# Two expert layers around a linear recurrence: the second layer's outputs added to the stored residual by accumulating scatters

## The chip, the cores and the metric

One core of a Trainium2 chip runs the whole program. The metric is the device time of one execution in microseconds. The kernel before took 563.17 us in the median of three runs (560.38 to 563.6).

## What is computed

The input is 4 sequences of 1024 tokens with 128 channels in float32. Three steps follow one another, each with a layer norm ahead of it and a residual around it: an expert layer with the better two of 8 experts for each token, a linear recurrence along the sequence, and the same expert layer again.

```python
x = x + 0.5 * moe(layernorm(x))
x = x + lru(layernorm(x))
x = x + 0.5 * moe(layernorm(x))

def moe(x):
    logits = x @ router_w.T + router_b
    topk_val, topk_idx = jax.lax.top_k(logits, 2)
    weights = jax.nn.softmax(topk_val, axis=-1)
    # for each of a token's two experts
    h = x @ w1[e].T + b1[e]; h1, h2 = split(h, 2)
    out = (silu(h1) * h2) @ w2[e].T + b2[e]
    return sum(weights * out)          # over the two experts
```

## The kernel before, in words

Each engine has a program of its own, written by hand, and semaphores tie them together; nothing reorders instructions, so the order in the code is the order on each engine. The residual stands in the on-chip buffer `xres` during the whole program. A layer number `f` (0 or 1) names the expert layer.

An expert layer works as follows. For each of the four sequences (`g`), PE makes the router's logits, DVE picks the two experts and works out a slot for each token and expert (`choose`, `row_weights`, `slots`). POOL then scatters the normalised tokens into a table in memory, `rows_dram[f]`, sorted by expert (`send_row`, line 436, 16 scatters of 128 rows for a sequence). A row is 130 words: the token as two float16 halves, its destination row (word `P`) and its weight (word `P + 1`). The table is cut into 39 tiles (`NTILE`) of 256 rows, each with rows of one expert; rows without a token are pads whose destination lies out of bounds, so a scatter leaves them out.

For each tile SP loads the tokens (transposed, line 363), destinations and weights (`meta`, line 367) and the bias (line 373). PE multiplies up and, two tiles later (`LAG`), down; ACT and DVE make the gated activation between them; ACT weights the result into one of eight buffers of `yout` (`weighted`, line 588). POOL sends these to memory (`send_y`, line 454): two scatters of 128 rows of 512 bytes, `r` = 0 and 1, to `y_dram[f]`, which has a row for each token and each of its two choices. The second scatter also waits until PE is three tiles further (`apart`). ACT fills a buffer again when the scatters of eight tiles before have landed (`s_ysent`). In the second layer two row scatters stand behind the outputs of each of tiles 0, 1 and 2, and eight behind those of each of tiles 5 and 6 (`BURSTS`). These are the rows of the third and fourth sequences that are still to be sent. The fourth sequence (`LATE`) is routed while the first 17 tiles (`KNOWN`), which hold the other three, are already being worked on.

When all outputs of a layer have landed, SP loads them back into `yin` (line 397, two loads of 512 KB for each sequence), DVE adds them to `xres` (`add_outputs`, line 967, two additions for each sequence), and, in the second layer alone, SP stores `xres` to `out` (line 402). The recurrence in between adds its part to `xres` on DVE in `add_recurrence` (line 1005) and raises `s_x2` for each sequence.

Of the kernel before, what the change touches and what calls it, by code (L numbers as in the profile page):

```python
# [6 lines left out]
FP32 = mybir.dt.float32  # L7
FP16 = mybir.dt.float16
I32 = mybir.dt.int32
ACT = mybir.ActivationFunctionType  # L10
ALU = mybir.AluOpType
AX = mybir.AxisListType.X

P = 128
BATCH, SEQ = 4, 1024
TOK = BATCH * SEQ
GT = SEQ // P
NE, HID, TOPK = 8, 512, 2
# [15 lines left out]
STEP = 4  # L34
BURSTS = {5: 8, 6: 8}
METAS, OUTS = 16, 8
# [4 lines left out]
LATE = BATCH - 1  # L41
# [4 lines left out]
KNOWN = WHOLE[LATE - 1]  # L46
# [8 lines left out]
def macaron_block(nc, x, nu_log, theta_log, b_re, b_im, c_re_t, c_im_t, d_vec, gamma_log,  # L55
                  router_t, router_b, w1_t, b1_t, w2_t, b2, out):
    ctx = ExitStack()
    with ctx:
# [3 lines left out]
        def sem(name):  # L62
            return ctx.enter_context(nc.semaphore(name))


        rows_dram = [nc.dram_tensor(f"rows{f}", [NE * REG + SLOT, ROWW], FP32, kind="Internal").ap() for f in range(2)]
        y_dram = [nc.dram_tensor(f"y{f}", [TOPK * TOK, P], FP32, kind="Internal").ap() for f in range(2)]


        xres = sb("xres", [P, BATCH, GT, P])  # L70
# [169 lines left out]
        s_cx = sem("s_cx")  # L240
        s_x2 = sem("s_x2")
        s_x3 = sem("s_x3")
        s_out = sem("s_out")

# [11 lines left out]
        def sent_before(f, tile, ring=STEP):  # L258

            count = lambda n: (n - tile % ring + ring - 1) // ring  # L260
            return f * count(NTILE) + count(tile)
# [51 lines left out]
        @block.sync  # L313
        def _(sp):
            route = [(rwt[:, :], router_t), (rbb[:, :], router_b.partition_broadcast(P))]
            small = [(b1g[:, :, :], b1_t), (b2b[:, 0, :], b2.partition_broadcast(2)),
                     (b_pow[:, 0, 0, :], b_re), (b_pow[:, 1, 0, :], b_im), (c_pow[:, 0, 0, :], c_re_t), (c_pow[:, 1, 0, :], c_im_t),
                     (vec[:, 0:1], nu_log), (vec[:, 1:2], theta_log), (vec[:, 3:4], d_vec), (vec[:, 2:3], gamma_log)]
            for g in range(BATCH):
                for c in range(2):  # L320
                    ts = slice(c * GT // 2, (c + 1) * GT // 2)
                    sp.dma_start(xres[:, g, ts, :], x[g].rearrange("(p t) d -> p t d", p=P)[:, ts, :])\
                        .then_inc(s_xin[g], 16)
                if g == 0:
                    for dst, src in route:
                        sp.dma_start(dst, src).then_inc(s_route, 16)
            for e in range(NE):
                if e == STAGED:
                    for dst, src in small:
                        sp.dma_start(dst, src).then_inc(s_small, 16)  # L330
                if e >= STAGED:

                    sp.wait_ge(s_wl, 2 * (e - STAGED + 1))
                sp.dma_start(wst[:, e % STAGED, 0:2 * HID], w1_t[:, e, :]).then_inc(s_w[e % STAGED], 16)
                sp.dma_start(wst[:, e % STAGED, 2 * HID:], w2_t[:, e, :]).then_inc(s_w[e % STAGED], 16)

            for f in range(2):

                sp.wait_ge(s_tab, f + 1)

                def pad(e):
                    row0 = sp.value_load(pad_i[0:1, f, e:e + 1], min_val=0, max_val=NE * REG - SLOT)
                    sp.dma_start(rows_dram[f][bass.ds(row0, SLOT), :].rearrange("(p r) w -> p r w", r=2),
                                 padrow[:, :, :]).then_inc(s_pad, 16)

                def pad_end():
                    sp.dma_start(rows_dram[f][NE * REG:NE * REG + SLOT, :].rearrange("(p r) w -> p r w", r=2),
                                 padrow[:, :, :]).then_inc(s_pad, 16)

                def load(t, n, dma):  # L350
                    if f > 0 and t == KNOWN:

                        sp.wait_ge(s_tab, 3)
                    row0 = sp.value_load(toff_i[0:1, f, t:t + 1], min_val=0, max_val=NE * REG)  # L354
                    if t in FIRST_OF:

                        sp.wait_ge(s_sent[FIRST_OF.index(t)], 16 * TOPK * GT * (f + 1))
                    if t == FIRST_OF[BATCH - 1]:

                        sp.wait_ge(s_pad, 16 * (NE + 1) * (f + 1))  # L360

                    wait(sp, s_up[HB - 1], n(1 - STEP))
                    sp.dma_start_transpose(xt_t[:, t % STEP, :, :], halves_dram[f][bass.ds(row0, SLOT), 0:2 * P])\  # L363
                        .then_inc(s_xt[t % STEP], 16)

                    wait(sp, s_ysent[t % OUTS], 32 * sent_before(f, t + OUTS - METAS, OUTS))
                    sp.dma_start(meta[:, t % METAS, :, :],  # L367
                                 rows_dram[f][bass.ds(row0, SLOT), P:].rearrange("(r p) w -> p r w", p=P))\
                        .then_inc(s_meta[t % STEP], 16)
                    expert = sp.value_load(tex_i[0:1, f, t:t + 1], min_val=0, max_val=NE - 1)  # L370

                    wait(sp, s_act[HB - 1], n(1 - STEP))
                    sp.dma_start(bias[:, t % STEP, :].unsqueeze(1), b1g[:, bass.ds(expert, 1), :])\  # L373
                        .then_inc(s_bias[t % STEP], 16)
                    if f > 0 and t == KNOWN - NE:

                        sp.wait_ge(s_ends, 1)
                    first_pad = STEP if f == 0 else KNOWN - NE
                    if first_pad <= t < first_pad + NE:
                        pad(t - first_pad)  # L380
                    if t == STEP:
                        pad_end()

                sp.wait_ge(s_b1u, 1)
                expert_tiles(f, load)

                if f == 0:
                    sp.wait_ge(s_turn, 1)
                for t in range(NTILE - OUTS, NTILE):
                    sp.wait_ge(s_ysent[t % OUTS], 32 * (sent_before(f, t, OUTS) + 1))  # L390
                for g in range(BATCH):
                    n = f * BATCH + g
                    if n >= 2:

                        sp.wait_ge(s_x1, n - 1)
                    for k in range(TOPK):
                        sp.dma_start(yin[:, n % 2, k, :, :],
                                     y_dram[f].rearrange("(k b p t) d -> k b p t d", k=TOPK, b=BATCH, p=P)[k, g])\
                            .then_inc(s_yin[n % 2][k], 16)
            for g in range(BATCH):  # L400
                sp.wait_ge(s_x1, BATCH + g + 1)
                sp.dma_start(out[g].rearrange("(p t) d -> p t d", p=P), xres[:, g, :, :]).then_inc(s_out, 16)
            sp.wait_ge(s_out, 16 * BATCH)


        @block.gpsimd
        def _(pool):
# [29 lines left out]
                    out=rows_dram[f], out_offset=bass.IndirectOffsetOnAxis(ap=slot_i[:, k, f, g, t:t + 1], axis=0),  # L437
                    in_=rows[:, k, g, t, :], in_offset=None).then_inc(s_sent[g], 16)

            last_row = pool.to_reg(TOPK * TOK - 1)  # L440

            def apart(t, j, n):

# [3 lines left out]
            def send_y(f, t, n):  # L447

                pool.wait_ge(s_yout, n(1))
                pool.sem_inc(s_ygo, 1)  # L450
                for r in range(2):
                    if r == 1:
                        apart(t, 0, n)
                    pool.indirect_dma_start(  # L454
                        out=y_dram[f],
                        out_offset=bass.IndirectOffsetOnAxis(ap=meta_i[:, t % METAS, r, 0:1], axis=0),
                        in_=yout[:, t % OUTS, r, :], in_offset=None, bounds_check=last_row,
                        oob_is_err=False).then_inc(s_ysent[t % OUTS], 16)

            for f in range(2):  # L460
                each = [(g, i) for g in range(BATCH) for i in range(TOPK * GT)]
# [181 lines left out]
        def _(dve):  # L643
# [8 lines left out]
            def linked(ins):  # L652

                count[0] += 1
                ins.then_inc(s_chain, 1)
                done = count[0]
                yield
                dve.wait_ge(s_chain, done)
# [110 lines left out]
            def row_weights(f, g):  # L769
                q = f * BATCH + g  # L770
                if (f, g) == (1, LATE):
                    yield from exponential(edif[:, q % 2, :], dif[:, q % 2, :], GT)
                else:

                    dve.wait_ge(s_edif, q + 1)
                yield from linked(V.tensor_scalar(den[:, :], edif[:, q % 2, :], 1.0, 2.0 * WS * WS, ALU.add, ALU.mult))
                yield from linked(V.reciprocal(wk[:, 0, :], den[:, :]))
                yield from linked(V.tensor_tensor(wk[:, 1, :], wk[:, 0, :], edif[:, q % 2, :], ALU.mult))
                for k in range(TOPK):
                    ins = V.tensor_copy(rows[:, k, g, :, P + 1:P + 2], wk[:, k, :].unsqueeze(2))  # L780
                yield from linked(ins)
# [329 lines left out]
            for f in range(2):  # L1111
# [31 lines left out]
                act_low(NTILE - 1, 1, lambda u: f * NTILE + NTILE - 1 + u)  # L1143
                for _ in late if f > 0 else tables:
                    pass
            for g in range(BATCH):
                add_outputs(1, g)


        @block.tensor  # L1150
# [263 lines left out]
```

## Time and profile before

| | us |
|---|---|
| median of three runs | 563.17 |
| the profiled execution, its own time | 563.79 |
| its span | 562.1 |
| busy in the span: PE, DVE, ACT, POOL | 451.9, 424.5, 359.0, 300.2 |

The engines are PE (matrix products), DVE (vectors), ACT (activations), POOL (which issues the indirect transfers) and SP (which issues the others). The profile is of one execution; its times are microseconds from the start of the span, and L454 is line 454 of the kernel before. A timeline row gives start, duration, engine, line, operation and, in brackets, how long the engine sat idle before it and what ended that. Landing is the time from the start of the issuing instruction until the transfer's semaphore is raised.

### The profile page before, as it was taken

The page shows a single profiled execution, that of the slowest core. Times are in us where ns is not written, and L with a number is a line of the kernel's source. Part 1 is how long each engine was busy: PE and PEld are TensorE (multiplying, and loading weights), DVE is VectorE, ACT ScalarE, POOL GpSimd, SP SyncE. Part 2 cuts the span into 40 slices and gives each one's busy share as a digit, 9 for nine tenths or more (in the row PEclk, how much of TensorE's full clock was granted, in tenths as well). Part 3 has the DMA queues.
Part 4 walks back from the last instruction along what each step waited for, and adds up shares of the span by engine and source line. Part 5 has one row for each costly group of instructions (what it writes and reads, how often), then busy time and mean ns, then how long its engine had stood idle before and what let it go on. Part 6 is the DMA issues. An engine that isn't in the chain of part 4 may idle for free.

```text
span 562.1 us, 15920 instructions
## 1 busy us (share of the span) xinstructions
PE 451.9 (80%) x4657; PEld 396.7 (71%) x4657; DVE 424.5 (76%) x1368; ACT 359.0 (64%) x797; POOL 300.2 (53%) x307
## 2 busy tenths in 40 slices
PE   7770269989899999987789986699987999999900
PEld 3660148768799999983689885488876889999900
DVE  8988658676879997744999998679965677777624
ACT  4896337666768877870607653578775688888700
POOL 1277876777864544551000477757677745454530
PEclk9555569999999999999688997799999999999955
DMA  8334433433334232316200011343344333333148
GB/s 286 121 110 141 114 83 93 102 98 93 73 76 72 54 65 57 64 25 218 82 1 1 31 53 49 86 80 86 78 107 93 87 70 66 58 66 63 28 147 301
DMA packets 94563, 50.27 MB, mean 89 GB/s; under 512 B 81902, under 2 KB 84720, under 8 KB 94484
## 3 DMA queue, kind: packets, MB, share of 16 engines
q1 hardware_dynamic: 85396, 32.31, 24.1%
q0 software_dynamic: 9088, 16.94, 9.7%
q8 instruction: 45, 0.74, 0.6%
q14 instruction: 34, 0.28, 0.2%
HBM read 17.25 MB, written 23.24 MB: 72 GB/s over the span
## 4 chain that ended last, share of the span: by engine, by line
PE 25%; SPq 24%; DVE 15%; POOL 13%; issue 11%; DMA 10%; ACT 2%; POOLq 0%; ACTq 0%; DVEq 0%
POOL rows L436 12%; SPq L363 9%; PE bank L1298 5%; PE bank L1300 5%; PE bank L1299 5%; SPq L373 4%; DMA xt_t<-rows 3%; SPq L367 3%; DMA yin<-y 3%; SPq L370 3%; SPq L354 3%; PE bank L1318 2%; PE bank L1319 2%; PE bank L1320 2%; DVE wst L1082 2%
## 5 line engine op out<-in xcount | busy, mean ns | idle before, releaser
L454 POOL DMA_INDIRECT y<-yout,meta x156 | 161.5, 1035 | 118.2 <-ACT yout L588 82.9
L1082 DVE SCALAR_TENSOR_TENSOR wst<-bank,bias,wst 128x256 f32<-128x256 f32 x312 | 148.6, 480 | 82.3 <-ACT wst L570 77.9
L1298 PE MATMUL bank<-xt_t,w1h 128*128 128x256 f16 x624 | 174.1, 279 | 43.1 <-DMA xt_t<-rows 26.9
L436 POOL DMA_INDIRECT rows<-rows,slot_i x128 | 136.6, 1068 | 120.6 <-DVE slot_i L797 81.6
L570 ACT ACTIVATE wst<-bank,bias 128x256 f32<-128x256 f32 x312 | 145.4, 474 | 74.5 <-PE bank L1300 42.0
L1299 PE MATMUL bank<-xt_t,w1h 128*128 128x256 f16 x624 | 173.9, 279 | 0.0
L1300 PE MATMUL bank<-xt_t,w1l 128*128 128x256 f16 x624 | 173.7, 278 | 0.0
L1318 PE MATMUL bank<-w2h,wst 128*128 x624 | 122.3, 220 | 1.0 <-DVE wst L1088 0.8
L1320 PE MATMUL bank<-w2h,wst 128*128 x624 | 120.2, 219 | 0.0
L1319 PE MATMUL bank<-w2l,wst 128*128 x624 | 120.2, 219 | 0.0
L1088 DVE TENSOR_TENSOR wst<-wst 128x512 f16<-128x512 f32 x156 | 107.8, 691 | 5.9 <-ACT wst L578 5.4
L578 ACT CAST wst<-wst 128x512 f16<-128x512 f32 x156 | 95.6, 613 | 16.1 <-DVE wst L1082 12.7
L1298 PEld LDWEIGHTS bank<-xt_t,w1h 128*128 x624 | 62.3, 100 | 53.1 <-issue 47.0
L491 ACT ACTIVATE xn<-xres,shift,rstd 128x128 f32<-128x128 f32 x96 | 38.2, 482 | 58.9 <-DVE shift L730 58.9
L1300 PEld LDWEIGHTS bank<-xt_t,w1l 128*128 x624 | 62.5, 100 | 8.6
L1318 PEld LDWEIGHTS bank<-w2h,wst 128*128 128x128 f16 x624 | 61.0, 98 | 7.8 <-issue 4.8
L1299 PEld LDWEIGHTS bank<-xt_t,w1h 128*128 x624 | 62.4, 100 | 4.7
L1319 PEld LDWEIGHTS bank<-w2l,wst 128*128 128x128 f16 x624 | 61.0, 98 | 2.3
L1320 PEld LDWEIGHTS bank<-w2h,wst 128*128 128x128 f16 x624 | 61.0, 98 | 0.0
L588 ACT ACTIVATE yout<-bank,meta 128x128 f32<-128x128 f32 x156 | 48.5, 364 | 2.7 <-PE bank L1320 2.6
L967 DVE TENSOR_TENSOR xres<-xres,yin 128x1024 f32<-128x1024 f32 x16 | 19.6, 1224 | 27.5 <-DMA yin<-y 27.0
L1162 PE MATMUL bank<-ident,xn 128*128 128x128 f32 x96 | 18.0, 329 | 10.3 <-ACT xn L491 10.0
(205 smaller groups left out, 509.3 us busy)
## 6 DMA issues: line engine op xcount, KB each, us to landing
yin<-y SPq DMA_DIRECT2D x16, 512.0 KB, 4.6
wst<-in_w_t SPq DMA_DIRECT2D x8, 512.0 KB, 5.0
y<-yout,meta POOLq DMA_INDIRECT x156, 2.4
rows<-padrow SPq DMA_DIRECT2D x18, 130.0 KB
xres<-in_x SPq DMA_DIRECT2D x8, 256.0 KB, 4.5
wst<-in_w_t SPq DMA_DIRECT2D x8, 256.0 KB, 5.7
rows<-rows,slot_i POOLq DMA_INDIRECT x128, 2.4
out<-xres SPq DMA_DIRECT2D x4, 512.0 KB, 6.9
```

Of the source, the lines that this page charges most:

```text
L436: pool.indirect_dma_start(out=rows_dram[f], out_offset=bass.IndirectOffsetOnAxis(ap=slot_i[:, k, f, g, t:t + 1], axis=0), in_=rows[:, k, g ...
L454: pool.indirect_dma_start(out=y_dram[f], out_offset=bass.IndirectOffsetOnAxis(ap=meta_i[:, t % METAS, r, 0:1], axis=0), in_=yout[:, t % OU ...
L570: nc.scalar.activation(gate[:, j, :], up_bank(f, t, j)[:, 0:SLOT], ACT.Silu, scale=1.0 / WS, bias=bias[:, t % STEP, j:j + 1]).then_inc(s_g ...
L578: nc.scalar.copy(acth[:, t % BUFS, 2 * half:2 * half + 2, :], act[:, 2 * half:2 * half + 2, :]).then_inc(s_acth[half], 1)
L1082: V.scalar_tensor_tensor(act[:, j, :], up_bank(f, t, j)[:, SLOT:], bias[:, t % STEP, HB + j:HB + j + 1], gate[:, j, :], ALU.add, ALU.mult) ...
L1088: V.tensor_tensor(actl[:, t % BUFS, h2, :], act[:, h2, :], acth[:, t % BUFS, h2, :], ALU.subtract).then_inc(s_actl[half], 1)
L1298: T.matmul(o, w1h[:, bass.ds(at, P)], xt_t[:, t % STEP, 0, :], start=True, stop=False)
L1299: T.matmul(o, w1h[:, bass.ds(at, P)], xt_t[:, t % STEP, 1, :], start=False, stop=False)
L1300: ins = T.matmul(o, w1l[:, bass.ds(at, P)], xt_t[:, t % STEP, 0, :], start=False, stop=True)
L1318: T.matmul(o, acth[:, t % BUFS, c, rs], w2h[:, bass.ds(at, P)], start=False, stop=False)
L1319: T.matmul(o, acth[:, t % BUFS, c, rs], w2l[:, bass.ds(at, P)], start=False, stop=False)
L1320: ins = T.matmul(o, actl[:, t % BUFS, c, rs], w2h[:, bass.ds(at, P)], start=False, stop=(c == HB - 1 and r == 1))
```

## The change

In the second layer the outputs don't go to a table of their own any more. The residual is stored to `out` beforehand: sequences 0 to 2 by SP between the layers, each when the recurrence has been added to it, and sequence 3 by SP behind the load of tile 4 (`base`). POOL's scatters then add to the rows of `out`. Both choices of a token go to the same row, so two tiles may hit one row, and the first scatter of a tile waits until both scatters of the tile before have landed. The first tile also waits for the stores of sequences 0 to 2, tile 17 for that of sequence 3. The destination of a token's second choice is set to the row of its first by one copy more on DVE for each sequence. The loads into `yin`, the additions and the stores at the end of the second layer go away; SP ends with the wait for the last eight tiles' scatters. The first layer stays as it was.

```diff
-        y_dram = [nc.dram_tensor(f"y{f}", [TOPK * TOK, P], FP32, kind="Internal").ap() for f in range(2)]
+        y_dram = nc.dram_tensor("y0", [TOPK * TOK, P], FP32, kind="Internal").ap()
+        sums = out.rearrange("b s d -> (b s) d")
...
+                def base(g):
+
+                    sp.wait_ge(s_x2, g + 1)
+                    sp.dma_start(out[g].rearrange("(p t) d -> p t d", p=P), xres[:, g, :, :]).then_inc(s_base[g], 16)
+
...
+                    if f > 0 and t == STEP:
+                        base(LATE)
...
-                for g in range(BATCH):
-                    n = f * BATCH + g
-                    if n >= 2:
-
-                        sp.wait_ge(s_x1, n - 1)
-                    for k in range(TOPK):
-                        sp.dma_start(yin[:, n % 2, k, :, :],
-                                     y_dram[f].rearrange("(k b p t) d -> k b p t d", k=TOPK, b=BATCH, p=P)[k, g])\
-                            .then_inc(s_yin[n % 2][k], 16)
-            for g in range(BATCH):
-                sp.wait_ge(s_x1, BATCH + g + 1)
-                sp.dma_start(out[g].rearrange("(p t) d -> p t d", p=P), xres[:, g, :, :]).then_inc(s_out, 16)
-            sp.wait_ge(s_out, 16 * BATCH)
+                if f == 0:
...
+                    for g in range(LATE):
+                        base(g)
...
-            last_row = pool.to_reg(TOPK * TOK - 1)
+            last_row = [pool.to_reg(TOPK * TOK - 1), pool.to_reg(TOK - 1)]
...
+                if f > 0:
+                    for g in range(BATCH):
+                        if t == (KNOWN if g == LATE else 0):
+
+                            pool.wait_ge(s_base[g], 16)
+                    if t > 0:
+
+                        pool.wait_ge(s_ysent[(t - 1) % OUTS], 32 * (sent_before(f, t - 1, OUTS) + 1))
...
-                        out=y_dram[f],
+                        out=sums if f else y_dram,
...
-                        in_=yout[:, t % OUTS, r, :], in_offset=None, bounds_check=last_row,
-                        oob_is_err=False).then_inc(s_ysent[t % OUTS], 16)
+                        in_=yout[:, t % OUTS, r, :], in_offset=None, bounds_check=last_row[f],
+                        oob_is_err=False, compute_op=ALU.add if f else ALU.bypass).then_inc(s_ysent[t % OUTS], 16)
...
+                if f > 0:
+                    V.tensor_copy(rows[:, 1, g, :, P:P + 1].bitcast(I32), dest_i[:, 0, g, :].unsqueeze(2))
...
-            for g in range(BATCH):
-                add_outputs(1, g)
```

POOL's queue in the second layer, before, from tile 5's outputs to tile 7's; `rows1` is the second layer's table, `y1` its outputs, and brackets name the semaphores that an instruction waits for:

```order
L454 DMA y1<-yout,meta 8192x128 [waits s_yout]
L454 DMA y1<-yout,meta 8192x128 [waits s_up0]
L436 DMA rows1<-rows,slot_i 35072x130 [waits s_slot,s_up1]
L436 DMA rows1<-rows,slot_i 35072x130 [waits s_up2]
L436 DMA rows1<-rows,slot_i 35072x130 x6
L454 DMA y1<-yout,meta 8192x128 [waits s_yout]
L454 DMA y1<-yout,meta 8192x128 [waits s_up0]
L436 DMA rows1<-rows,slot_i 35072x130 [waits s_row,s_up1]
L436 DMA rows1<-rows,slot_i 35072x130 [waits s_up2]
L436 DMA rows1<-rows,slot_i 35072x130 x6
L454 DMA y1<-yout,meta 8192x128 [waits s_yout]
L454 DMA y1<-yout,meta 8192x128 [waits s_up0]
```

The same place on POOL after the change, where the outputs go to `out_0`:

```order
L468 DMA out_0<-yout,meta 4096x128 [waits s_yout,s_ysent4]
L468 DMA out_0<-yout,meta 4096x128 [waits s_up0]
L442 DMA rows1<-rows,slot_i 35072x130 [waits s_slot,s_up1]
L442 DMA rows1<-rows,slot_i 35072x130 [waits s_up2]
L442 DMA rows1<-rows,slot_i 35072x130 x6
L468 DMA out_0<-yout,meta 4096x128 [waits s_yout,s_ysent5]
L468 DMA out_0<-yout,meta 4096x128 [waits s_up0]
L442 DMA rows1<-rows,slot_i 35072x130 [waits s_row,s_up1]
L442 DMA rows1<-rows,slot_i 35072x130 [waits s_up2]
L442 DMA rows1<-rows,slot_i 35072x130 x6
L468 DMA out_0<-yout,meta 4096x128 [waits s_yout,s_ysent6]
L468 DMA out_0<-yout,meta 4096x128 [waits s_up0]
```

Nothing has moved on POOL; each tile's first scatter has a second wait, for the scatters of the tile before (`s_ysent4` is tile 4's).

SP's queue at the end of the program, before, from the last tile's load of `meta`:

```order
L367 DMA meta<-rows1 128x2x2
L370 TENSOR_LOAD tex_i
L370 ISA x2
L373 ISA [waits s_act3]
L373 DMA bias<-b1g 128x8
L397 DMA yin<-y1 128x1024 [waits s_ysent4,s_ysent3,s_ysent5,s_ysent2,s_ysent6,s_ysent1,s_x1,s_ysent0,s_ysent7]
L397 DMA yin<-y1 128x1024
...
L397 DMA yin<-y1 128x1024 [waits s_x1]
L397 DMA yin<-y1 128x1024
L402 DMA out_0<-xres 128x1024 [waits s_x1] x4
L58 UNCONDITIONAL_BRANCH [waits s_out]
```

And after the change:

```order
L373 DMA meta<-rows1 128x2x2
L376 TENSOR_LOAD tex_i
L376 ISA x2
L379 ISA [waits s_act3]
L379 DMA bias<-b1g 128x8
L58 UNCONDITIONAL_BRANCH [waits s_ysent3,s_ysent4,s_ysent2,s_ysent5,s_ysent1,s_ysent6,s_ysent0,s_ysent7]
```

Eight loads and four stores are gone from SP's end; the wait for the last eight tiles' scatters stays and now stands ahead of the program's end.

## Rows read from the trace of the kernel before

**Rows 1.** Busy time by engine in stretches; us, then PE to POOL, clock, DMA
```profile
core 0 of [0], span 562.1 us
core 0: us, PE busy (x) PEld busy (x) DVE busy (x) ACT busy (x) POOL busy (x), PEclk, DMA share, GB/s
541.00:562.10 21.10, 0.00 (x0) 0.00 (x0) 9.80 (x8) 0.00 (x0) 0.00 (x0) 0.50 0.83 299
```

**Rows 2.** The chain that ended last, its end: start, duration, engine or transfer
```profile
538.62 2.15 DMA y<-yout,meta
...
541.79 5.74 DMA yin<-y
...
557.10 1.22 DVE xres L967
```

**Rows 3.** Line 402, the stores of out: duration in ns, first and last start
```profile
L402 SPq DMA_DIRECT2D out<-xres x4: 332/381/430, 550.9 to 558.4; - x4
...
DMA to landing us min/median/max: 3.3/6.9/7.6
```

**Rows 4.** Timeline of POOL in the second layer, around tiles 6 to 16
```profile
422.17 0.96 POOL L436 DMA_INDIRECT rows<-rows,slot_i  x1 [0.30 <-issue]
423.43 1.00 POOL L454 DMA_INDIRECT y<-yout,meta  x1 [0.30 <-issue]
...
450.57 0.98 POOL L454 DMA_INDIRECT y<-yout,meta  x1 [1.88 <-ACT yout L588]
```

**Rows 5.** Timeline of ACT, the outputs of tile 7 and of tile 30
```profile
403.90 0.62 ACT L588 ACTIVATE yout<-bank,meta 128x128 f32<-128x128 f32 x2
...
506.33 0.63 ACT L588 ACTIVATE yout<-bank,meta 128x128 f32<-128x128 f32 x2
```

**Rows 6.** Timeline of POOL, the two scatters of tile 30 and the next
```profile
507.75 0.98 POOL L454 DMA_INDIRECT y<-yout,meta  x1 [1.80 <-ACT yout L588]
509.04 0.98 POOL L454 DMA_INDIRECT y<-yout,meta  x1 [0.30 <-issue]
511.82 0.98 POOL L454 DMA_INDIRECT y<-yout,meta  x1 [1.80 <-ACT yout L588]
```

**Rows 7.** Line 454 in 425 to 450, then landings in 475-500 and 500-541
```profile
L454 POOL DMA_INDIRECT y<-yout,meta x17: 982/993/1474, 424.7 to 447.7; - x17
...
DMA to landing us min/median/max: 2.4/2.5/2.6
...
DMA to landing us min/median/max: 2.5/2.6/2.8
...
DMA to landing us min/median/max: 2.1/2.1/2.1
```

**Rows 8.** Timeline from 313 us: copies on DVE and the scatter they release
```profile
313.11 0.24 DVE L780 COPY rows<-wk 128x8 f32<-128x8 f32 x2
313.26 0.24 DVE L797 CAST slot_i<-slot 128x8 int32<-128x8 f32 x2
...
313.77 0.96 POOL L436 DMA_INDIRECT rows<-rows,slot_i  x1 [58.61 <-DVE slot_i L797]
```

**Rows 9.** Timeline of SP's queue: a pad, the next tile's load, tile 17's load
```profile
371.68 0.59 SPq L347 DMA_DIRECT2D rows<-padrow  x1
372.97 1.22 SPq L363 DMA_TRANSPOSE xt_t<-rows  x1
...
437.02 1.27 SPq L363 DMA_TRANSPOSE xt_t<-rows  x1
```

**Rows 10.** DMA queues (packets, MB, share of 16 engines) and issues (us to landing)
```profile
q0 software_dynamic: 9088, 16.94, 9.7%
...
y<-yout,meta POOLq DMA_INDIRECT x156, 2.4
...
rows<-rows,slot_i POOLq DMA_INDIRECT x128, 2.4
...
rwt<-in_router_t SPq DMA_DIRECT2D x1, 4.0 KB, 2.6
```

More of the change, by code:

```diff
@@ L242, in macaron_block @@
         s_x3 = sem("s_x3")
-        s_out = sem("s_out")
+        s_base = [sem(f"s_base{g}") for g in range(BATCH)]
         order = [("ffn", 0, g) for g in range(BATCH)]
@@ L390, in _ @@
                     sp.wait_ge(s_ysent[t % OUTS], 32 * (sent_before(f, t, OUTS) + 1))
-                for g in range(BATCH):
-                    n = f * BATCH + g
-                    if n >= 2:
-                        sp.wait_ge(s_x1, n - 1)
-                    for k in range(TOPK):
-                        sp.dma_start(yin[:, n % 2, k, :, :],
-                                     y_dram[f].rearrange("(k b p t) d -> k b p t d", k=TOPK, b=BATCH, p=P)[k, g])\
-                            .then_inc(s_yin[n % 2][k], 16)
-            for g in range(BATCH):
-                sp.wait_ge(s_x1, BATCH + g + 1)
-                sp.dma_start(out[g].rearrange("(p t) d -> p t d", p=P), xres[:, g, :, :]).then_inc(s_out, 16)
-            sp.wait_ge(s_out, 16 * BATCH)
+                if f == 0:
+                    for g in range(BATCH):
+                        if g >= 2:
+                            sp.wait_ge(s_x1, g - 1)
+                        for k in range(TOPK):
+                            sp.dma_start(yin[:, g % 2, k, :, :],
+                                         y_dram.rearrange("(k b p t) d -> k b p t d", k=TOPK, b=BATCH, p=P)[k, g])\
+                                .then_inc(s_yin[g % 2][k], 16)
+                    for g in range(LATE):
+                        base(g)
         @block.gpsimd
@@ L450, in send_y @@
                 pool.sem_inc(s_ygo, 1)
+                if f > 0:
+                    for g in range(BATCH):
+                        if t == (KNOWN if g == LATE else 0):
+                            pool.wait_ge(s_base[g], 16)
+                    if t > 0:
+                        pool.wait_ge(s_ysent[(t - 1) % OUTS], 32 * (sent_before(f, t - 1, OUTS) + 1))
                 for r in range(2):
```

## The prediction

> **What bounds the kernel now.** I read the chain that ended last first, from its end backwards. The last scatter of the second layer's outputs starts on POOL at 538.62 us and lands 2.15 us later, at 540.77; then only loads of yin, additions on DVE and stores of out follow [rows 2]. In that stretch PE and ACT do nothing and the transfers move 299 GB/s [rows 1]. The four stores of out take 3.3 to 7.6 us to land [rows 3], and the span ends at 562.1 [rows 1]. So 562.1 - 540.8 = 21.3 us at the end hang on the outputs taking a detour through memory. That is all that the change can win.
>
> Next I looked at what the change puts a wait into: POOL's queue in the second layer. POOL falls behind there, because after the scatters of tiles 5 and 6 it also sends eight rows each. Tile 7's outputs are ready on ACT at 403.90 + 0.62 = 404.5 [rows 5], but its first scatter starts at 423.43 [rows 4]. A scatter that ACT releases starts 0.79 us after ACT's end (506.96 to 507.75) [rows 5, 6], so tile 7 is 423.4 - 405.3 = 18.1 us late. Before, that costs nothing: from there POOL sends one scatter after the other, 17 of them from 424.7 to 447.7 at 23.0 / 16 = 1.44 us apart [rows 7], 2.9 us per tile, and at 450.57 it waits for ACT again [rows 4]. From then on a tile takes 4.07 us (507.75 to 511.82), the rhythm of PE and ACT, and POOL idles 1.80 us in each [rows 6]. The second layer's end is PE's end plus a short tail of three tiles' scatters.
>
> **The change, part by part.**
>
> *The end.* Removed: 8 loads of yin, 8 additions on DVE and 4 stores, together the 21.3 us above; what is left is SP's wait for the last scatters. I keep 0.4 us for it: the last store started at 558.4; with the shortest landing, 3.3 us, it was there at 561.7, and the span ended 0.4 after that [rows 1, 3].
>
> *The wait of a tile's scatters for the last tile's landing.* This is the large term. A tile's round on POOL becomes: first scatter, second scatter, landing of the second, wake-up. The second starts 1.29 us after the first where POOL is undisturbed (507.75 to 509.04) [rows 6] and 1.44 in the stretch to 448 [rows 7]. From a scatter's start to its landing the medians are 2.5 us up to 450, 2.6 up to 500, and 2.1 in the last stretch, when no tile is loaded any more [rows 7]; I use 2.5 and 2.1. For the wake-up I take a row scatter that DVE released: slot_i's last copy ends at 313.50, POOL starts at 313.77, 0.27 later [rows 8]. So even a scatter that costs what it costs today gives a round of 1.29 + 2.5 + 0.27 = 4.06 us, just the 4.07 at which tiles come. There is no slack left, and the 18.1 us of tile 7 are never made up. Added up from 423.4: six rounds of 4.21 (with 1.44) to 448.7, eighteen of 4.06 to 521.8, seven of 3.66 (with 2.1) to 547.4, which is tile 38's first scatter; 1.29 + 2.15 more give the last landing at 550.8. With the 0.4 the span would end at 551.2, 10.9 us sooner than before: half of the gain is given back by the wait alone. Queued behind the waiting scatter are POOL's later scatters only, from tile 7 on; ACT waits for them through the ring of eight yout buffers, which a lag of eight tiles (some 33 us) uses up. For tiles 0 to 4 the lag is too small to matter, and the row sends of tiles 5 and 6 stand behind a landing wait each, about 1 us late at most, against 12 us between their last start at 422.17 [rows 4] and tile 17's load at 437.02 [rows 9].
>
> *Adding instead of writing.* No row of before shows an accumulating transfer. Call e what one tile's round is longer by, for both scatters. From tile 7 on there are 31 rounds and the last landing, so the span ends at 551.2 + 32 e, and e = 10.9 / 32 = 0.34 us is the break-even. From below: a scatter that also reads its target can't be quicker than the same one that doesn't, so e is 0 or more. From above: a whole small load from memory, 2.6 us from issue to landing [rows 10], in line before each write, and a second pass of POOL over the 128 addresses, 0.98 us more for each of two scatters: 2.6 + 1.96 = 4.6 us. In between I build it from the plain scatter, the nearest row. POOL's queue kept 16 engines busy for 9.7% of the span, 54.5 us, for 156 + 128 scatters [rows 10]: 0.19 us each. Reading 64 KB back takes that again: 0.19. Of a landing of 2.1, 0.98 is POOL's own time [rows 6] and 0.19 the moving, which leaves 0.93 for one read on the way, one write and its receipt; I take half of it for the read of the target: 0.47. And POOL's own time hardly depends on the form (0.96 for a row scatter, 0.98 for one with a bounds check [rows 4]); 0.05 more for each of two scatters. So e = 0.19 + 0.47 + 0.10 = 0.76 us, and 32 e = 24.3 us. By the Trainium skill ("DMA: Bandwidth & Descriptors", section "Latency and other measured facts") a memory access takes 0.2 us on average and 2 us under high load; an estimate from it alone is e = 0.2 to 2, a span of 558 to 615. No run here shows it.
>
> *Stores of the residual.* Three stores of 512 KB go out while SP waits between the layers; the fourth stands behind tile 4's load, right after a pad of 130 KB at 371.68 [rows 9]. At up to 7.6 us it lands by about 380, long before tile 17 asks for it, and may hold up the next tile load at 372.97 by some 3 us; from tile 7 on POOL is the later one by 18 us, so I count 0. Without that cover it would be those 3 us.
>
> *One copy more on DVE* per group of rows: a copy of the same shape takes 0.24 / 2 = 0.12 us [rows 8], for four groups 0.5 us, counted as 0 because most of it falls between instructions of the chain interleaved with it; the end of the range has room for it.
>
> **Sum.** 551.2 + 24.3 = 575.5 us of span. The profiled execution took 563.79 for a span of 562.1, 1.7 outside it, and lies 0.1% above the median of 563.17. So 577.2, written 577 us: 2.5% slower.
>
> **Rivals.** About 1% is what a measurement of this kernel can tell from no change: 557.5 to 568.8 us, e from 0.14 to 0.50.
>
> First, on the other side: the read of the target is hidden. The engine reads source and target at once and the wait for the receipt covers the difference, so that only a little moving time is left, e below 0.14. What speaks for it: of 2.1 us of landing only 0.19 is moving. Against: the target lies in memory and the source on the chip, and nothing in the trace reads memory in that little. The time is 553 to 557, from the point e = 0.14 on faster by over 1%; I name 555. The Trainium skill has a rule that gives this ("DMA: Bandwidth & Descriptors", section "Anatomy of one DMA", on the path of GpSimd): about 2.0 us fixed plus the bytes over 436 GB/s. By it 64 KB land in 2.15 us, and the trace agrees where nothing else moves (2.1 [rows 7]); 64 KB more would be an estimate of 0.15 us, hence 557.7.
>
> Second, a draw: the read costs 0.14 to 0.50, the gain at the end and the slower rounds cancel, 557.5 to 568.8, named 563.
>
> Third, much slower: POOL itself makes a second pass over its 128 addresses for the reads, up to 0.98 us in each scatter. Then e = 0.19 + 1.96 = 2.15 and the span ends at 551.2 + 69 = 620, the time 622; half a pass gives about 1.6 with the read's latency, 604. Above e of about 0.6 the lag uses up the yout ring before the end, so ACT and PE stall as well; that adds nothing, since POOL is the bound by then. For it speaks that POOL writes each address itself; against it that a bounds check adds only 0.02.
>
> That the change doesn't do what it says I give nothing: the order of POOL's and SP's queues shows the waits and the missing end.
>
> **How the numbers follow.** Hidden read 0.20; draw 0.20; the forecast, e from 0.5 to 1.2 (569 to 591), 0.38; much slower 0.22. The low end is e = 0, 552.9, written 552, since the hidden read holds too much chance to be left out; the high end is e = 1.97, 551.2 + 63 + 1.7 = 616, which leaves a part of the full second pass outside. The forecast's own range is 569 to 591. Faster 0.20, same 0.20, slower 0.60.
>
> **What would show it right or wrong.** Right: after tile 7 POOL's scatters are released by landings, never again by ACT; first scatters stand 4.7 to 5 us apart from 450 to 520 where they stood 4.07 apart; PE ends near 535 to 542, long before the last landing; DVE has no additions at the end. An accumulating scatter lands about 3.2 us after its start. Wrong: POOL catching up with ACT again before tile 38 (then e is about 0), scatters of clearly more than 1.03 us on POOL (third rival), or PE ending late for a reason of its own, such as a tile load held up by the fourth store.

## The result and the profile after

The changed kernel takes 617.35 us in the median of four runs (613.63 to 619.58), the kernel before 561.77 on the same chip: a ratio of 1.098, with a 95% interval of 1.091 to 1.106. It is slower, as forecast, but by 9.8% instead of 2.5%, and 617 lies just above the range's upper end of 616. The profiled execution took 613.63 us with a span of 611.8.

The timeline of POOL after the change, at the places of [rows 4] and [rows 6] (line 468 is the scatter of outputs, now into `out`):

```profile
396.13 1.56 POOL L468 DMA_INDIRECT out<-yout,meta  x1 [2.07 <-DMA out<-yout,meta]
...
401.72 1.85 POOL L468 DMA_INDIRECT out<-yout,meta  x1 [2.17 <-DMA out<-yout,meta]
...
429.13 0.95 POOL L442 DMA_INDIRECT rows<-rows,slot_i  x1 [0.30 <-issue]
430.39 1.69 POOL L468 DMA_INDIRECT out<-yout,meta  x1 [0.30 <-issue]
432.38 1.89 POOL L468 DMA_INDIRECT out<-yout,meta  x1 [0.30 <-issue]
436.60 1.55 POOL L468 DMA_INDIRECT out<-yout,meta  x1 [2.33 <-DMA out<-yout,meta]
...
453.70 1.55 POOL L468 DMA_INDIRECT out<-yout,meta  x1 [2.31 <-ACT yout L602]
...
555.54 1.55 POOL L468 DMA_INDIRECT out<-yout,meta  x1 [1.93 <-DMA out<-yout,meta]
557.39 1.55 POOL L468 DMA_INDIRECT out<-yout,meta  x1 [0.31 <-issue]
560.98 1.55 POOL L468 DMA_INDIRECT out<-yout,meta  x1 [2.03 <-DMA out<-yout,meta]
...
602.45 1.55 POOL L468 DMA_INDIRECT out<-yout,meta  x1 [1.44 <-DMA out<-yout,meta]
604.30 1.55 POOL L468 DMA_INDIRECT out<-yout,meta  x1 [0.30 <-issue]
```

Three things are to be seen. The idle time ahead of a tile's first scatter is ended by a landing ("DMA out<-yout,meta"), where it was ACT in [rows 6]. From tile 8 on 30 of the 31 rows name a landing. The one at 453.70, tile 11, names ACT, but tile 11's outputs had been ready since 422.0; the event that fell there was tile 17's, at 453.4. A round takes 5.44 us (555.54 to 560.98), where tiles came every 4.07. And a scatter occupies POOL for 1.55 us, where it was 0.98. Tiles 4 and 5, the first two rows, already wait about 2.1 us for a landing each. Tile 7 starts at 430.39 (423.43 in [rows 4]) and tile 38 at 602.45: 31 rounds in 172.1 us, 5.55 on average.

Line 468 in 541 to 575, the page's row on the queue of POOL's transfers, and the drains at the end of the programs (line 58; duration in ns, first and last start; SP's COMPARE_BRANCH is the first thing that it does after its last wait), to be read beside [rows 7] and [rows 10]:

```profile
L468 POOL DMA_INDIRECT out<-yout,meta x13: 1552/1554/1597, 541.2 to 573.8; - x13
...
DMA to landing us min/median/max: 3.3/3.3/3.3
...
q0 software_dynamic: 17824, 16.95, 14.5%
...
L58 PEldq DRAIN  x1: 1385/1385/1385, 557.7 to 557.7; - x1
L58 POOLq DRAIN  x1: 9373/9373/9373, 602.2 to 602.2; - x1
L58 SPq COMPARE_BRANCH  x1: 41/41/41, 607.1 to 607.1; - x1
```

A landing takes 3.3 us where 2.1 to 2.6 stood in [rows 7]. PE is through at 557.7 + 1.4 = 559.1 (the end of its drain), some 48 us before the last landing, which SP sees at 607.1. And the program doesn't end there: POOL's drain lasts until 602.2 + 9.4 = 611.6, which is the end of the span. The old end, 541 to 562 in [rows 1], is gone as it was meant to be; what remains after 559.1 is POOL, but for two late outputs of ACT, the last at 566.8. In the kernel before, the same drain was hidden:

```profile
L58 POOLq DRAIN  x1: 12952/12952/12952, 535.7 to 535.7; - x1
```

It ended at 548.7, under the loads and stores that lasted until 562.1.

### The profile page after: what moved, and what is told of

Same layout as the page of the kernel before. It is cut to its first block, busy times and chain, and to the rows that moved or that the text cites. A ratio compares the mean times of both kernels' runs of the same rounds, so it can differ in the third digit from the quotient of the medians.

```text
span 611.8 us, 15907 instructions
## 1 busy us (share of the span) xinstructions
PE 458.0 (75%) x4657; PEld 396.4 (65%) x4657; DVE 413.3 (68%) x1364; ACT 354.2 (58%) x797; POOL 342.4 (56%) x307
## 3 DMA queue, kind: packets, MB, share of 16 engines
q0 software_dynamic: 17824, 16.95, 14.5%
## 4 chain that ended last, share of the span: by engine, by line
POOL 24%; PE 22%; issue 18%; SPq 15%; DVE 10%; DMA 9%; ACT 2%; POOLq 0%; DVEq 0%; ACTq 0%
POOL out L468 12%; POOL rows L442 11%; SPq L369 5%; PE bank L1312 4%; PE bank L1314 4%; PE bank L1313 4%; DMA out<-yout,meta 2%; DMA xt_t<-rows 2%; SPq L373 2%; SPq L379 2%; PE bank L1333 2%; PE bank L1332 2%; PE bank L1334 2%; SPq L376 2%; SPq L360 2%
## 5 line engine op out<-in xcount | busy, mean ns | idle before, releaser
L584 ACT ACTIVATE wst<-bank,bias 128x256 f32<-128x256 f32 x312 | 143.6, 475 | 62.7 <-DMA bias<-b1g 31.0
L468 POOL DMA_INDIRECT out<-yout,meta x78 | 123.8, 1588 | 84.7 <-DMA out<-yout,meta 67.9
L1332 PE MATMUL bank<-w2h,wst 128*128 x624 | 124.7, 221 | 1.8 <-DVE wst L1104 1.2
L1334 PE MATMUL bank<-w2h,wst 128*128 x624 | 121.3, 220 | 0.0
L1104 DVE TENSOR_TENSOR wst<-wst 128x512 f16<-128x512 f32 x156 | 107.6, 690 | 10.6 <-ACT wst L592 10.4
L468 POOL DMA_INDIRECT y<-yout,meta x78 | 81.1, 1040 | 57.2 <-ACT yout L602 40.5
L602 ACT ACTIVATE yout<-bank,meta 128x128 f32<-128x128 f32 x156 | 48.5, 363 | 42.5 <-issue 38.0
L1326 PE MATMUL bank<-b2p,ones 128*128 x156 | 21.7, 221 | 18.5 <-ACT yout L602 18.5
```

What stands on the lines that cost most here:

```text
L468: pool.indirect_dma_start(out=sums if f else y_dram, out_offset=bass.IndirectOffsetOnAxis(ap=meta_i[:, t % METAS, r, 0:1], axis=0), in_=yo ...
L584: nc.scalar.activation(gate[:, j, :], up_bank(f, t, j)[:, 0:SLOT], ACT.Silu, scale=1.0 / WS, bias=bias[:, t % STEP, j:j + 1]).then_inc(s_g ...
L1104: V.tensor_tensor(actl[:, t % BUFS, h2, :], act[:, h2, :], acth[:, t % BUFS, h2, :], ALU.subtract).then_inc(s_actl[half], 1)
L1332: T.matmul(o, acth[:, t % BUFS, c, rs], w2h[:, bass.ds(at, P)], start=False, stop=False)
L1334: ins = T.matmul(o, actl[:, t % BUFS, c, rs], w2h[:, bass.ds(at, P)], start=False, stop=(c == HB - 1 and r == 1))
```

## The experiments

The theory after the result: every tile costs a round of first scatter, second scatter, landing and wake-up, so all that an adding scatter takes longer is paid in each round; and a drain of POOL stands behind the last one. The rivals: the adds are dear wherever they stand; or the wait itself is dear; or the adds' transfers hold up the tile loads.

**The wait without the adds.**

```diff
-                        oob_is_err=False, compute_op=ALU.add if f else ALU.bypass).then_inc(s_ysent[t % OUTS], 16)
+                        oob_is_err=False, compute_op=ALU.bypass).then_inc(s_ysent[t % OUTS], 16)
```

> The changed kernel with plain writes in place of the adds; the wait for the last tile's landing stays (left out: the second layer's outputs overwrite rows of the output instead of being added). Theory (the wait gives every tile a round of scatter, scatter, landing, wake-up, and what the add itself costs comes on top of each round): a round of 4.06 to 4.21 us, the last landing at 549 to 552, then POOL's drain of 4 to 8 us, time 555 to 561. Rival (the wait costs nothing by itself, only the add is dear): POOL catches up with ACT, last landing at 541, time 550.

Measured: 569.57 us, ratio 1.012 (1.002 to 1.023). Its POOL, at the end of the work:

```profile
550.35 0.98 POOL L468 DMA_INDIRECT out<-yout,meta  x1 [1.39 <-DMA out<-yout,meta]
551.64 0.98 POOL L468 DMA_INDIRECT out<-yout,meta  x1 [0.30 <-issue]
554.01 0.98 POOL L468 DMA_INDIRECT out<-yout,meta  x1 [1.39 <-DMA out<-yout,meta]
555.30 0.98 POOL L468 DMA_INDIRECT out<-yout,meta  x1 [0.30 <-issue]
557.67 0.98 POOL L468 DMA_INDIRECT out<-yout,meta  x1 [1.39 <-DMA out<-yout,meta]
558.96 0.98 POOL L468 DMA_INDIRECT out<-yout,meta  x1 [0.30 <-issue]
```

The rival is out: POOL never catches up with ACT. It starts each tile from tile 7 on 19 to 24 us after ACT has finished that tile (six rows between 499 and 532 name ACT, but for outputs of later tiles), and the last rounds are the 3.66 us of the forecast (554.01 to 557.67). But the time lies 9 us above what the theory said. Tile 7 starts at 427.57 instead of 423.4, the 31 rounds to 557.67 take 4.20 us on average instead of 4.00, and the landing is seen at 561.2 instead of 550.8. The rows of the middle show why the rounds are longer:

```profile
L468 POOL DMA_INDIRECT out<-yout,meta x11: 982/983/1468, 449.8 to 474.2; - x11
...
DMA to landing us min/median/max: 3.4/3.5/3.6
```

The same stretch (450 to 475) in the kernel before:

```profile
L454 POOL DMA_INDIRECT y<-yout,meta x12: 980/982/1031, 450.6 to 472.4; - x12
...
DMA to landing us min/median/max: 2.2/2.5/2.7
```

Here a plain scatter took 3.5 us to land, where the same operation took 2.5 before, and some held POOL for up to 1.47. What lengthens them there was not tried. Then comes a drain that ends at 569.0.

**The adds without the wait.** Both choices have rows of their own, so no two scatters hit one row. The two more stores for each sequence are left out of the lines shown.

```diff
-        sums = out.rearrange("b s d -> (b s) d")
+        sums = nc.dram_tensor("y1", [TOPK * TOK, P], FP32, kind="Internal").ap()
...
-                    if t > 0:
-                        pool.wait_ge(s_ysent[(t - 1) % OUTS], 32 * (sent_before(f, t - 1, OUTS) + 1))
```

> The changed kernel with the adds but without the wait between tiles: both choices have rows of their own in a table that SP fills from the residual (two more stores for each sequence), so that no two scatters hit one row (left out: the outputs don't reach the output tensor). Theory (the dear thing is that a landing stands in each round): POOL spends 3.7 us on a tile, less than the 4.07 at which tiles come; tile 38's first scatter at 541 to 546, last landing at 546 to 551, then a drain of 4 to 8, time 552 to 560. Rival (adds are dear wherever they stand, on POOL or in the transfers): rounds stay above 5 us, time over 600. Second rival (the adds' transfers hold up the tile loads): PE ends after 545 and the time is 565 to 590.

Measured: 562.20 us, ratio 0.999 (0.994 to 1.004). From 448 on POOL goes from one scatter to the next without a pause, 1.73 us each and 0.30 between, until the work of the tiles ends at 533:

```profile
529.60 1.74 POOL L468 DMA_INDIRECT y<-yout,meta  x1 [0.31 <-issue]
531.64 1.73 POOL L468 DMA_INDIRECT y<-yout,meta  x1 [0.30 <-issue]
533.67 1.55 POOL L468 DMA_INDIRECT y<-yout,meta  x1 [0.30 <-issue]
535.53 1.56 POOL L468 DMA_INDIRECT y<-yout,meta  x1 [0.30 <-ACT yout L602]
```

The first rival falls: a tile costs 4.07 us here, not 5.44. The second falls too: PE's own drain starts at 534.2, against 533.4 before. The theory's 552 to 560 was 2 us low, because from 448 on a scatter holds POOL for 1.73 us and not for 1.55, so a tile takes 2 x (1.73 + 0.30) = 4.06 us and the backlog isn't worked off; tile 38 starts at 550.43 instead of 541 to 546. That other engines are at work is not enough to explain the 1.73, since beside the same work a scatter took 1.55 to 1.60 in the changed kernel. DVE's rows in this run show more:

```profile
499.06 1.73 POOL L468 DMA_INDIRECT y<-yout,meta  x1 [0.30 <-issue]
500.27 0.48 DVE L1096 SCALAR_TENSOR_TENSOR wst<-bank,bias,wst 128x256 f32<-128x256 f32 x1 [0.52 <-ACT wst L584]
501.10 1.74 POOL L468 DMA_INDIRECT y<-yout,meta  x1 [0.30 <-issue]
502.31 0.48 DVE L1096 SCALAR_TENSOR_TENSOR wst<-bank,bias,wst 128x256 f32<-128x256 f32 x1 [0.50 <-ACT wst L584]
```

The scatters end at 500.79 and 502.84, 0.04 and 0.05 us after DVE's instruction of line 1096 has ended (500.75 and 502.79), and nearly all from 448 to 531 end so. In the run with the wait alone most of the long plain scatters (1.03 to 1.50 us) end 0.45 to 0.47 us after such an instruction. That points to POOL being held until DVE is done; no run varied it, so this is not shown as the cause.

**Neither adds nor wait.** The worth of the removed end by itself.

```diff
-        sums = out.rearrange("b s d -> (b s) d")
+        sums = nc.dram_tensor("y1", [TOPK * TOK, P], FP32, kind="Internal").ap()
...
-                    if t > 0:
-                        pool.wait_ge(s_ysent[(t - 1) % OUTS], 32 * (sent_before(f, t - 1, OUTS) + 1))
...
-                        oob_is_err=False, compute_op=ALU.add if f else ALU.bypass).then_inc(s_ysent[t % OUTS], 16)
+                        oob_is_err=False, compute_op=ALU.bypass).then_inc(s_ysent[t % OUTS], 16)
```

> Neither adds nor the wait: plain scatters into a table of their own as before, the residual stored early, no loads, additions and stores at the end (left out: the outputs don't reach the output tensor). This is what the removed end is worth by itself. Theory (POOL's drain at the end of the program, hidden under the old end, comes to light): last landing at 541, POOL's drain ends at about 549, time 550 to 552. Rival (the forecast's 0.4 us between landing and end): time 543.

Measured: 551.30 us, ratio 0.980 (0.971 to 0.989). The last landing and the drain:

```profile
L58 POOLq DRAIN  x1: 12955/12955/12955, 536.7 to 536.7; - x1
L58 SPq COMPARE_BRANCH  x1: 41/41/41, 541.9 to 541.9; - x1
```

SP sees the last landing at 541.9, the drain ends at 549.7, and the span at 549.9. The removed end was therefore worth 12 us (563.28, the runs of before in this comparison, less 551.30), not the 21.3 of the forecast: the other 8 or 9 were a drain that had been running beneath it.

With these four times the change can be taken apart. From 551.3, the wait alone adds 18.3 us, the adds alone 10.9, both together 66.0. The 37 us or so that neither has alone are what the theory says: with the wait, each scatter's extra time stands in a chain of 31 rounds.

**Half of each row's bytes.**

```diff
-        sums = out.rearrange("b s d -> (b s) d")
+        sums = out.rearrange("b s (h d) -> (b s h) d", h=2)
...
-                        in_=yout[:, t % OUTS, r, :], in_offset=None, bounds_check=last_row[f],
+                        in_=yout[:, t % OUTS, r, 0:P // 2] if f else yout[:, t % OUTS, r, :], in_offset=None, bounds_check=last_row[f],
```

> The changed kernel with adds of 256 bytes a row instead of 512 (left out: half of the channels). Theory (POOL's 0.57 us more for each adding scatter are spent on the 128 addresses, and the landing after it on latency): POOL's time stays at 1.55, the round at 5.2 to 5.5, time 608 to 618. Rival (the add's cost goes by bytes): POOL's time about 1.27 and a round of 4.8, time 590 to 600.

Measured: 612.31 us, ratio 1.088 (1.079 to 1.098); POOL's time stayed at 1.55 us, the landing in 541 to 575 fell from 3.3 to 3.1. Between 512 and 256 bytes a row the price of the add hardly goes by bytes, as the theory said.

**Half of the rows, adding and plain.** The first edit, made to the changed kernel; the second run has plain scatters as well.

```diff
-                        out_offset=bass.IndirectOffsetOnAxis(ap=meta_i[:, t % METAS, r, 0:1], axis=0),
-                        in_=yout[:, t % OUTS, r, :], in_offset=None, bounds_check=last_row[f],
+                        out_offset=bass.IndirectOffsetOnAxis(ap=meta_i[0:P // 2 if f else P, t % METAS, r, 0:1], axis=0),
+                        in_=yout[0:P // 2 if f else P, t % OUTS, r, :], in_offset=None, bounds_check=last_row[f],
```

> The changed kernel with scatters of 64 rows instead of 128, adds and wait as they are (left out: half of the rows of every tile). Theory (POOL's 0.57 us more for an adding scatter are spent address by address): POOL's time falls from 1.55 to 0.9 to 1.1 and the added part, against the plain scatter of 64 rows, to 0.25 to 0.32; a round of 4.2 to 4.6, time 575 to 590. Rival (a fixed price of an adding instruction): the added part stays at 0.5 to 0.6, POOL's time at 1.2 to 1.3, time 595 to 605.

> The wait with plain scatters of 64 rows (left out: half of the rows, and the rest overwrites instead of adding). It gives the plain scatter's price by address. Theory: POOL's time 0.55 to 0.75 for 64 rows; rounds of 3.2 to 3.8, so POOL catches up with ACT, last landing at 541 to 543, drain as with plain scatters (9 us after the last scatter's end), time 550 to 553. Rival (most of the 0.98 is fixed): POOL's time 0.85 or more, time 555 to 565.

Measured: 609.16 us adding (ratio 1.081, 1.074 to 1.089) and 562.48 plain (1.000, 0.995 to 1.005). Line 468 in 541 to 575 of the one and of the other:

```profile
L468 POOL DMA_INDIRECT out<-yout,meta x14: 1397/1402/1602, 541.1 to 572.7; - x14
```

```profile
L468 POOL DMA_INDIRECT out<-yout,meta x4: 906/907/908, 540.3 to 545.0; - x4
```

My theory of a price by address is refuted. A plain scatter takes 0.98 us for 128 rows and 0.91 for 64: 1.1 ns a row. An adding one takes 1.55 and 1.40: 2.3 ns a row. So of the 0.57 us that an add costs, about 0.42 are spent on the instruction and 1.2 to 1.3 ns on each row, by a straight line through these two sizes; other sizes were not tried. Scatters are dear on POOL mostly by their number. The rival of a fixed price comes nearer, but its figures were too low as well (1.2 to 1.3 us on POOL, 595 to 605). The plain run missed its theory's 550 to 553 and is in its rival's 555 to 565, with 0.91 us on POOL: its landings, with medians of 3.2 (425 to 450) and 2.9 us (450 to 475), kept POOL at least 10.7 us behind ACT to the end.

**Two targets in turn.** Even tiles add to `out`, odd ones to a second table, and a tile waits for the tile before the last.

```diff
+        other = nc.dram_tensor("y1", [TOK, P], FP32, kind="Internal").ap()
...
-                        pool.wait_ge(s_ysent[(t - 1) % OUTS], 32 * (sent_before(f, t - 1, OUTS) + 1))
+                        pool.wait_ge(s_ysent[(t - 2) % OUTS], 32 * (sent_before(f, t - 2, OUTS) + 1))
...
-                        out=sums if f else y_dram,
+                        out=(sums, other)[t % 2] if f else y_dram,
```

> The changed kernel with two targets in turn: even tiles add to the output, odd ones to a table that SP also fills from the residual, so a tile waits for the tile before the last (left out: the odd tiles' outputs don't reach the output). Theory (what costs is a landing in series with every tile's scatters): the wait stands but is over when POOL gets there, rounds of 3.7 to 4.1, time 558 to 568, as without any wait. Rival (a wait for a landing costs its wake-up and order wherever it stands): rounds over 4.5, time over 580.

Measured: 560.91 us, ratio 0.999 (0.995 to 1.002), as without any wait. Its POOL:

```profile
458.56 1.55 POOL L470 DMA_INDIRECT y<-yout,meta  x1 [0.30 <-issue]
460.42 1.55 POOL L470 DMA_INDIRECT y<-yout,meta  x1 [0.30 <-issue]
462.28 1.55 POOL L470 DMA_INDIRECT out<-yout,meta  x1 [0.30 <-issue]
464.14 1.55 POOL L470 DMA_INDIRECT out<-yout,meta  x1 [0.30 <-DMA y<-yout,meta]
```

From tile 7 on no first scatter waits longer than the usual 0.30. A wait for a landing costs nothing as long as other scatters fill the time; it is the landing of the tile just before that costs. This run settles the theory against the rival that waits are dear in themselves.

**The drain.**

```diff
+            last = NTILE - 1
+            pool.wait_ge(s_ysent[last % OUTS], 32 * (sent_before(1, last, OUTS) + 1))
```

> The run with neither adds nor wait, and POOL also waits for the last scatter's landing before its program ends (left out: the outputs don't reach the output tensor). Theory (what POOL's drain waits for runs from the last scatter, so waiting first costs nothing): the drain still ends 9.1 us after the last scatter's end, time 550.5 to 552. Rival (the drain is work of its own that starts when POOL gets to it): it ends 9 us or more after the landing, time 553 to 557.

Measured: 550.23 us, ratio 0.980 (0.970 to 0.989). The two runs, 548.39 and 552.07, lie about where the theory put the time, and below the 553 to 557 of the rival. But two runs so far apart don't decide a difference of 2 us, and the trace does:

```profile
L58 POOLq DRAIN  x1: 9051/9051/9051, 541.0 to 541.0; - x1
```

POOL comes to it with nothing outstanding and it still takes 9.05 us from there, to 550.05, which is 10.4 us after the last scatter's end (539.68) where the theory had 9.1. In the run with neither, it ended 9.0 us after the last scatter's end (540.62 to 549.66). So the drain is time of POOL's own, after its last instruction. The theory that it runs from the last scatter is refuted. The rival holds in what the drain does, and missed the time because waiting for the landing delayed POOL by only 1.3 us.

The runs that are faster than the kernel before leave the adds out, so no version here beats it at the same work. Adds free of the wait already cost what the old end cost (562.2 and 560.9), and they would still have a second table to add.

## Why the forecast had the direction and not the size

*The end.* "That is all that the change can win", 21.3 us, and the 0.4 us kept behind the last landing were wrong. I looked at what the end did and not at what ran beneath it. POOL's drain takes 4.5 us beyond the landing with adds (607.1 to 611.6) and 8 with plain scatters; the removed end was worth 12.

*The wait.* The mechanism was right: no slack, POOL behind from tile 7 on, released by landings to the end, PE long done. The term was under-sized: 31 rounds of 4.20 with plain scatters where I had 4.00, and 4.2 us of later start where I had allowed 1 us at most. I had read the landings from rows in which no one waited for them.

*The add.* This is the step that failed most. "POOL's own time hardly depends on the form ... 0.05 more for each of two scatters": it is 0.57, so 1.14 a round instead of 0.10. I took the bounds check's 0.02 for the price of an add, which it says nothing about, and gave the rival that has POOL work longer the smaller chance. My own sign for that rival, scatters of clearly more than 1.03 us on POOL, is what came. The other part, 0.66 us from POOL's end to the landing, came out much lower. At the quiet end POOL waits 1.44 us for the landing with adds (602.45) and 1.39 with plain scatters (557.67 in the run with the wait alone), so there the read of the target costs about 0.05. On average over the 31 rounds the adds make 5.55 - 4.20 = 1.35, of which 1.14 are POOL's own, so about 0.2 is left for it. The forecast of an add that lands about 3.2 us after its start came true (3.3 in 541 to 575) by luck: too much for the read made up for too little on POOL.

*The sum*, on the profiled execution: 611.8 - 575.5 = 36.3 us too low. Tile 7 starts 7.0 later than I had it; 31 rounds of 5.55 instead of the 4.76 that I had on average (4.00 + 0.76) give 24.5 (6.2 of it from the wait's rounds, the rest from the add); from tile 38's start to the landing 4.6 instead of 4.2, 0.4; and the end is 4.7 instead of 0.4, 4.3. That makes 36.2.

*The rivals.* The hidden read had the read about right and fell on POOL's time. The Trainium skill's rule that I gave with it ("DMA: Bandwidth & Descriptors", section "Anatomy of one DMA") doesn't hold for these scatters: from 425 us on their medians by stretch are 3.0 to 3.6 us, the shortest is 2.7, and halving the bytes changed 0.2. "Much slower" had the right engine but the wrong mechanism, a pass over the addresses. Its 0.98 us for a full pass and 0.49 for half of one enclose the 0.57 measured, nearer to the half; that the full pass's 622 lies nearest to 617 is luck, since 7.0 us of later start and 4.3 of drain, which it didn't have, stand in for rounds shorter than it said. The yout ring did run full, as said for such e. Before, ACT stood idle ahead of its outputs (line 588) for 2.7 us in total; now (line 602) it is 42.5, and the first of these waits, at tile 20, names the landing:

```profile
466.37 0.62 ACT L602 ACTIVATE yout<-bank,meta 128x128 f32<-128x128 f32 x2 [1.29 <-DMA out<-yout,meta]
```

PE ends 25 us later than before (559.1 against 534.0), at no cost, because POOL is the bound. The edits counted as nothing stayed so as far as the trace shows: the four early stores land in 2.6 to 3.2 us.

## What to carry to other kernels

When a change makes transfers wait for one another, add up the whole round (issue, issue, landing, wake-up) and compare it with the rhythm of the work; once it exceeds that, every fraction of a microsecond in it is paid as often as the loop runs. Let the order wait for something older than the last transfer: a wait that other work fills was free here. And before counting an end as gained, look for what ends beneath it, in the queues' rows too and not only in the chain.

## What I had not expected of the hardware

An adding scatter of 128 rows held POOL for 1.55 us against 0.98, most of the difference per instruction (0.42 us, from two sizes) and not per row. It also went out in other packets: 17,824 on POOL's queue after against 9,088 before [rows 10], so (17824 - 9088) / 78 = 112 more for each of 78 adding scatters, 144 in place of 32; the run with 64 rows has 12,832, which makes 80. That is one for each row and 16 more.

POOL's drain at the end of the program took 9.05 us with nothing outstanding after plain scatters; after adds of 128 rows it ended 5.7 us after the last scatter (605.85 to 611.6), and after scatters of 64 rows 9.7 (adding) and 10.4 us (plain). Why these differ stays open.

A chain of adds without waits kept exactly the tiles' rhythm, 1.73 us for a scatter, and fell to 1.55 when DVE's last work came at 533. Scatter after scatter ended 0.03 to 0.05 us after an instruction of DVE's line 1096, in the run with two targets as well (there line 1100, from 468 on). In the changed kernel, whose scatters wait for landings, a scatter took no more than 1.60 from 436 on.
